# Second cross-attention with the logits computed once and turned probabilities, and the last batch's layer norm of the first cross-attention moved into the local attention's first steps

## The chip, the cores and the metric

The kernel runs on one core of a Trainium2 chip. The metric is the device time of one execution in microseconds (us). Engines: TensorE (PE, with its weight loads PEld), VectorE (DVE), ScalarE (ACT), GpSimd (POOL) and SyncE (SP), which starts the transfers. A difference under 0.5% (9.7 us) can't be told from no change here.

## What is computed

Four batches of 512 tokens of 128 numbers pass through four blocks; each block reads the layer norm of the stream and adds its result to the stream.

```python
x = x + cross_attention(layernorm(x), ctx)        # part a
x = x + six_local_attention_layers(layernorm(x))  # part b: windows of 32, 16 heads, each with a gated FFN
x = x + second_cross_attention(layernorm(x), ctx) # part c
x = x + mixture_of_8_experts(layernorm(x))        # part c
```

The second cross-attention, of which the change rewrites the softmax (77 context rows, 16 heads of 8 numbers):

```python
qp = q @ Wq.T
scores = qp @ kv.T ; idx = argmax(scores, -1)
mem = kv[idx] ; mk, mv = split(mem @ Wkv.T, 2)
logits = (qh @ mk.T) / sqrt(8)
attn = softmax(logits, -1)
out = (attn @ mv) @ Wc.T
```

Since every row of `mem` is one of the 77 context rows, the kernel counts how often each row is picked (a one-hot matrix, summed by PE) and works on 77 keys with their counts.

## The kernel before

The program has three parts, each a block in which the five engines run their own instruction lists in order and meet through semaphores; between the parts all engines meet. The residual stream lies in `residual` (X), the normalised stream in `stream` (XS), both 128 partitions wide with 16 tiles of 128 tokens. A tile is called u (0 to 15), a batch b has four.

Part a (`cross_attention`) ends, for every batch, with `residual(b)` on DVE (the sum, then the statistics), `second(b)` on POOL (variance plus epsilon, then the power -1/2) and `stream(b)` on DVE (subtract the mean, multiply). Batch 3 is last: nothing else is left when its chain runs.

Part b (`windowed_layers`) begins with small fills and tables. POOL waits for four transfers (`const_in`, two of them the query and key scales, two the layer norm's gain and bias) before it makes the rotary table of layer 0. PE's `enter(b)` transposes the normalised stream of batch b; `enter(3)` comes only in the third turn of four tiles. Each engine follows a written list (`PE_TURN`, `ACT_TURN`, `DVE_TURN`, `POOL_TURN`). Near its end part b also prepares batch 0 of the second cross-attention (the functions `first_...`): `first_queries` on ACT copies the queries from PSUM three times, whole and in two halves, `low` and `high`.

Part c (`gathered_mixture`) is a software pipeline over tiles. In iteration u, PE computes the logits of tile u+1 (L2449, four groups of four heads, 128 tokens by 308, one PSUM bank each), the probabilities of tile u, the attended values of tile u-1 (L2472, and `by_token` L2480, which turns them back to tokens) and the output of tile u-2. The softmax works so: DVE takes the maximum of each head over 77 keys (`highest`, L2094). PE turns these negative maxima (L2455), ACT copies them (L1935) into rows of `low` and `high`, which hold the queries of half of the heads each. PE then computes the logits a second time, turned (keys on the partitions) and with the maximum already subtracted, since the maxima stand among the rows of the product (`probs_t`, L2464, four groups). ACT takes the exponential as it reads them from PSUM (L1941) into `probs_t`. DVE's `shares` (L2100, L2105) divides by the sum.

Beside this every batch has pieces that share the bank of the fourth logits group (`bk_p`): `normed`, `queries`, `scores`, `counts` for the next batch, and `route`, `affine`, `rank` for tiles that are done. A piece in iteration u waits on PE until DVE has read the logits of tile u+1:

```python
def piece_bank(kind, b):
    wait(pe, piece_done, nth[kind, b] - 1)
    if (kind, b) in where:
        pe.wait_ge(lmax_done, 4 * min(where[kind, b] + 2, NT))
```

DVE's order in an iteration is: `highest(u+1)`, `residual(u-2)`, the statistics of finished tiles, `best` (the argmax and the one-hot, L2064), `keys`, `shares(u-1)`, and the rest. After `highest`, `best` and `shares` of one iteration PE still has `counts`, the last group of `probs_t` and `attended_tt` (L2485, which needs `shares(u-1)`) before the next logits.

## Time and profile before

| | |
|---|---|
| median of 3 runs | 1940.81 us (1939.25 to 1948.31) |
| profiled execution | 1946.22 us, its span 1944.0 us |
| part a, from the span's start to the meeting | 0 to 68.1 us |
| part b | 68.1 to 1715.1 us |
| part c, cross-attention iterations 0 to 15 | 1715.1 to about 1868 us |
| part c, the rest | to 1944.0 us |
| mean granted clock of PE | 0.973 |

The profile gives for every engine the time in which it worked; a share near 1 tells where work may bound a stretch, and the timeline and the waits tell what an idle engine waited for. "Granted clock" is the share of PE's 2.4 GHz that it was given: 1.00 or 0.50.

### The profile page before, as it was taken

To read this page: it belongs to the slowest core of one execution; us is meant where nothing else is said; L and a number is where in the kernel's file an instruction comes from. 1 tells how busy PE (TensorE), PEld (TensorE's weight loads), DVE (VectorE), ACT (ScalarE), POOL (GpSimd) and SP (SyncE) were. 2 spreads that over 40 slices of the span, in tenths; PEclk is the share of its full clock that TensorE was granted. 3 is DMA by queue.
4 is the path that set the end of the run, shared out by engine and by line. 5 is a ranking of instruction groups with operands and counts; after the bars stand their busy time and mean duration, and the time that the engine had idled before them with its cause. 6 is when DMAs were issued, how large, how long until landed. Compare 5 with 4: busy or idle time off the path is not lost. (4 is left out here: it accounts for less than half of the span.)

```text
span 1944.0 us, 78927 instructions
## 1 busy us (share of the span) xinstructions
PE 1819.9 (94%) x32815; PEld 1274.1 (66%) x32815; DVE 1433.7 (74%) x2623; ACT 1140.1 (59%) x2387; POOL 1438.3 (74%) x1838
## 2 busy tenths in 40 slices
PE   7689999999999999999999999999999999789878
PEld 6356667666666666666666766666666666566668
DVE  4587777877787778778777877888778878355556
ACT  2266566656666665666566666656666666334434
POOL 2588779878888888888788888888888879222334
PEclk9799999999999999999999999999999999889979
DMA  3111311111311113111122111121111101030012
GB/s 103 30 52 44 103 49 49 52 45 48 102 54 49 41 47 103 53 45 52 48 67 85 51 41 45 35 88 33 28 35 37 39 24 36 10 100 1 20 44 67
DMA packets 60837, 99.93 MB, mean 51 GB/s; under 512 B 15848, under 2 KB 35065, under 8 KB 58643
## 3 DMA queue, kind: packets, MB, share of 16 engines
q1 hardware_dynamic: 58978, 91.72, 16.3%
q8 instruction: 262, 4.29, 1.0%
q0 software_dynamic: 1504, 3.17, 0.5%
q14 instruction: 93, 0.75, 0.1%
HBM read 44.50 MB, written 21.45 MB: 34 GB/s over the span
## 5 line engine op out<-in xcount | busy, mean ns | idle before, releaser
L1332 PE MATMUL b_bank_proj<-layer_weights,b_stream_t 128*128 128x512 f32 x1152 | 593.7, 617 | 12.5 <-DVE b_plain_moved L1128 9.3
L1128 DVE TENSOR_TENSOR b_plain_moved<-b_bank_proj,b_rope 128x1024 f32<-128x1024 f32 x384 | 467.4, 1221 | 110.3 <-ACT b_squares L962 107.0
L871 POOL TENSOR_TENSOR b_rotated<-b_plain_moved 128x1024 f32<-128x1024 f32 x192 | 453.7, 2363 | 46.5 <-DVE b_plain_moved L1128 46.5
L886 POOL TENSOR_TENSOR b_rotated<-b_rotated,b_inv_norm 128x1024 f32<-128x1024 f32 x192 | 365.5, 1904 | 15.2 <-POOL b_inv_norm L882 0.2
L962 ACT ACTIVATE b_squares<-b_bank_proj 128x512 f32<-128x512 f32 x384 | 229.3, 597 | 248.3 <-PE b_bank_proj L1332 245.3
L1332 PEld LDWEIGHTS b_bank_proj<-layer_weights,b_stream_t 128*128 128x128 f32 x1152 | 188.7, 192 | 115.3 <-issue 53.2
L1134 DVE TENSOR_REDUCE b_norm<-b_squares 128x16 f32<-128x1024 f32 x192 | 232.2, 1209 | 42.7 <-ACT b_squares L962 42.5
L1340 PEld LDWEIGHTS b_bank_shared<-const_tables,b_rotated 128*128 128x128 f32 x1536 | 181.5, 143 | 72.9 <-issue 68.8
L1340 PE MATMUL b_bank_shared<-const_tables,b_rotated 128*128 128x128 f32 x1536 | 213.1, 277 | 3.4 <-POOL b_rotated L886 1.6
L891 POOL TENSOR_TENSOR b_probs<-b_probs,b_inv_sum 128x512 f32<-128x512 f32 x192 | 200.8, 1049 | 14.4 <-DVE b_inv_sum L1149 14.3
L1406 PEld LDWEIGHTS b_bank_shared<-b_attended_t,layer_weights 128*128 128x128 f32 x1536 | 184.2, 193 | 24.9 <-issue 23.2
L1406 PE MATMUL b_bank_shared<-b_attended_t,layer_weights 128*128 128x128 f32 x1536 | 188.5, 276 | 1.6 <-ACT b_attended_t L999 1.6
L1140 DVE TENSOR_REDUCE b_max<-b_bank_scores 128x8 f32<-128x512 f32 x192 | 130.0, 677 | 80.4 <-PE b_bank_scores L1365 80.2
L999 ACT ACTIVATE b_attended_t<-b_bank_shared 128x512 f32<-128x512 f32 x192 | 106.7, 595 | 98.9 <-PE b_bank_shared L1394 97.4
L969 ACT ACTIVATE b_v<-b_bank_proj 128x512 f32<-128x512 f32 x192 | 114.7, 597 | 83.3 <-PE b_bank_proj L1332 80.6
L1365 PE MATMUL b_bank_scores<-b_k_t,b_q_t 64*32 64x64 f32 x12288 | 146.6, 224 | 14.5 <-issue 11.8
L1365 PEld LDWEIGHTS b_bank_scores<-b_k_t,b_q_t 64*32 64x32 f32 x12288 | 140.4, 105 | 24.5 <-issue 16.1
L1394 PEld LDWEIGHTS b_bank_shared<-b_probs_t,b_v_shifted 64*64 64x64 f32 x6144 | 98.4, 134 | 71.9 <-issue 71.1
L1437 PE MATMUL b_bank_proj<-b_normed_t,layer_weights 128*128 128x512 f32 (+1 forms) x288 | 144.1, 616 | 1.1 <-issue 0.6
L1142 DVE TENSOR_TENSOR b_bank_scores<-b_bank_scores,b_max 128x512 f32<-128x512 f32 x192 | 134.3, 700 | 6.6
L1394 PE MATMUL b_bank_shared<-b_probs_t,b_v 64*64 64x32 f32 x6144 | 115.2, 221 | 25.5 <-issue 25.5
L1375 PEld LDWEIGHTS b_bank_shared<-const_tables,b_probs 128*128 128x128 f32 x768 | 94.4, 143 | 64.3 <-issue 58.5
(367 smaller groups left out, 2896.7 us busy)
## 6 DMA issues: line engine op xcount, KB each, us to landing
b_v_shifted<-b_v SPq DMA_DIRECT2D x192, 192.0 KB, 2.4
sorted_rows<-sorted_rows SPq DMA_DIRECT2D x66, 258.0 KB, 3.2
layer_weights<-L_ffn_Wqkv SPq DMA_DIRECT2D x6, 1536.0 KB
b_v_shifted<-b_v SPq DMA_DIRECT2D x72, 128.0 KB, 3.0
layer_weights<-L_ffn_Wo SPq DMA_DIRECT2D x6, 512.0 KB
c_sorted_in<-sorted_rows SPq DMA_DIRECT2D x23, 129.0 KB, 2.2
layer_weights<-L_ffn_w SPq DMA_DIRECT2D x8, 256.0 KB, 5.8
c_w<-L_ffn_w SPq DMA_DIRECT2D x8, 256.0 KB, 5.7
```

The lines of the kernel that those rows point to most:

```text
L871: nc.gpsimd.tensor_tensor(out=turned[:, k, :], in0=pm[:, k, 0, :], in1=pm[:, k, 1, :], op=ALU.add).then_inc(add_done, 1)
L886: nc.gpsimd.tensor_tensor(out=tk, in0=tk, in1=repeat_last(rn[:, k, :], DH), op=ALU.mult).then_inc(rope_done, 1)
L891: nc.gpsimd.tensor_tensor(out=p, in0=p, in1=repeat_last(share[:, b, :], LOOK), op=ALU.mult).then_inc(p_done, 1)
L962: nc.scalar.activation(squares[:, (c % 2) * 512:(c % 2) * 512 + 512], bk_proj[c % 2][:, :], ACT.Square).then_inc(sq_done, 1)
L1128: nc.vector.tensor_tensor(to, src.to_broadcast(shape), tab.to_broadcast(shape), ALU.mult).then_inc(mul_done, 1)
L1134: nc.vector.tensor_reduce(ss[:, k, :], squares[:, :].rearrange("p (a h c) -> p h a c", a=2, h=HEADS), AX.XY, ALU.add).then_inc(ss_done, 1)
L1332: nc.tensor.matmul(out, xs[:, b, t * P:(t + 1) * P], w, start=True, stop=True).then_inc(proj_full, 1)
L1340: last = nc.tensor.transpose(bank[:, n * P:(n + 1) * P], turned[:, g // 2, at:at + P], ident)
L1365: last = nc.tensor.matmul(bk_s[r][to, at:at + LOOK], qT[rows, u % 2, p, w, :], kT[rows, p, t * P + w * WIN:t * P + w * WIN + LOOK], start= ...
L1394: last = nc.tensor.matmul(banks[r][h * HALF:(h + 1) * HALF, p * HALF + w * WIN:p * HALF + (w + 1) * WIN], (V2, V)[w][rows, t, head * DH:(h ...
L1406: last = nc.tensor.matmul(bank[:, 0:P], weights(l, W_O + n * P, P), OT[:, u % 2, n, :], start=(n == 0), stop=(n == PAIRS - 1))
L1437: nc.tensor.matmul(bk_proj[c % 2][0:w, :], weights(l, W_UP + at, w), xnT[:, :], start=True, stop=True).then_inc(up_full, 1)
```

## The change

1. Last layer norm of part a. Statistics, power and normalisation of batch 3 leave part a. In part b DVE's first instructions are the statistics, POOL does the two small ones after its fills, and DVE normalises after its tables. `enter(3)` waits for it. POOL's wait before the rotary table is now for the two scale transfers alone.
2. Softmax of part c. `highest` on DVE now also subtracts the maximum from each group of logits (PSUM) and writes the differences to a new tile `raised` in SBUF. ACT takes the exponential there, in place. PE transposes the four groups (16 transposes a tile), and ACT copies them from PSUM to `probs_t`. The turned maxima, their copies, `low` and `high`, their fills and the half copies of the queries are gone. A piece's wait (`lmax_done`) now ends with the subtraction.

```diff
 def highest(u):                                   # DVE
-    wait(dve, max_full, u - 1)
+    wait(dve, pT_full, 4 * (u - 1))
     for n, g in enumerate((0, 2, 1, 3)):
         dve.wait_ge(lg_full, 4 * u + n + 1)
-        nc.vector.tensor_reduce(nm[:, u % 2, at:at + GROUP], split(bk_l[g][:, 0:GROUP * CTX], CTX), AX.X, ALU.max,
-                                negate=True).then_inc(lmax_done, 1)
+        group = split(bk_l[g][:, 0:GROUP * CTX], CTX)
+        largest = nm[:, u % 2, g * GROUP:(g + 1) * GROUP]
+        nc.vector.tensor_reduce(largest, group, AX.X, ALU.max, negate=True).then_inc(max_done, 1)
+        dve.wait_ge(max_done, 4 * u + n + 1)
+        nc.vector.tensor_tensor(split(raised[:, u % 2, g, :], CTX), group, repeat_last(largest, CTX),
+                                ALU.add).then_inc(lmax_done, 1)
-def highest(u):                                   # ACT
-    act.wait_ge(max_full, u + 1)
-    for a in range(2):
-        last = nc.scalar.activation(stack(a, b)[maxes[a], t * P:(t + 1) * P], bk_l[0][maxes[a], 384:384 + P], ACT.Copy)
-    last.then_inc(max_done, 1)
+def exponent(u):                                  # ACT, in its place
+    for n, g in enumerate((0, 2, 1, 3)):
+        act.wait_ge(lmax_done, 4 * u + n + 1)
+        nc.scalar.activation(raised[:, u % 2, g, :], raised[:, u % 2, g, :], ACT.Exp).then_inc(raised_done, 1)
 def probs_t(u, q):                                # ACT
-    nc.scalar.activation(pT[:, u % 2, q, :], bk_t[q % 2][0:CTX, :], ACT.Exp).then_inc(pT_done, 1)
+    nc.scalar.activation(pT[:, u % 2, (0, 2, 1, 3)[q], :], bk_t[q % 2][0:CTX, :], ACT.Copy).then_inc(pT_done, 1)
 def probs_t(u, q):                                # PE
-    if q == 0:
-        pe.wait_ge(max_done, u + 1)
+    g = (0, 2, 1, 3)[q]
+    pe.wait_ge(raised_done, 4 * u + q + 1)
     wait(pe, pT_done, 4 * u + q - 1)
     for n in range(GROUP):
-        last = nc.tensor.matmul(bk_t[q % 2][0:CTX, n * P:(n + 1) * P], kbd[:, b % 2, a, h, :],
-                                stack(a, b)[:, t * P:(t + 1) * P], start=True, stop=True)
+        last = nc.tensor.transpose(bk_t[q % 2][0:CTX, n * P:(n + 1) * P], raised[:, u % 2, g, n * CTX:(n + 1) * CTX], ident)
@@ first_queries, and queries(b) alike
-    nc.scalar.activation(front.queries, bank[:, :], ACT.Copy)
-    nc.scalar.activation(front.low[sides[0], :], bank[sides[0], :], ACT.Copy)
-    nc.scalar.activation(front.high[sides[1], :], bank[sides[1], :], ACT.Copy).then_inc(fq_done, 1)
+    nc.scalar.activation(front.queries, bank[:, :], ACT.Copy).then_inc(fq_done, 1)
```

On PE, in part c, iteration 3 before, with one piece (`normed`, L2386); `c_low_queries_max` and `layer_weights` are where the stacked queries lie:

```order
L2449 MATMUL c_bank_logits<-c_keys_by_head,c_queries_t 128x308 x4
L2464 MATMUL c_bank_turned<-layer_weights,c_keys_by_head 77x128 x4
L2489 MATMUL c_bank_out<-layer_weights,c_attended_tt 128x128
L2464 MATMUL c_bank_turned<-layer_weights,c_keys_by_head 77x128 x4
L2472 MATMUL c_bank_attended<-c_probs_t,layer_weights 32x512 x4
L2464 MATMUL c_bank_turned<-layer_weights,c_keys_by_head 77x128 x4
L2480 MATMUL c_bank_out<-const_tables,c_attended_t 128x128 x4
L2386 MATMUL c_bank_logits<-const_tables,c_normed 128x128 x4
L2455 MATMUL c_bank_logits<-const_tables,c_neg_max 128x128
L2464 MATMUL c_bank_turned<-layer_weights,c_keys_by_head 77x128 x4
L2485 MATMUL c_bank_out<-const_tables,c_attended 128x128
```

The same iteration on PE after the change:

```order
L2458 MATMUL c_bank_logits<-c_keys_by_head,c_queries_t 128x308 x4
L2467 MATMUL c_bank_turned<-const_tables,c_raised 77x128 x4
L2491 MATMUL c_bank_out<-layer_weights,c_attended_tt 128x128
L2467 MATMUL c_bank_turned<-const_tables,c_raised 77x128 x4
L2474 MATMUL c_bank_attended<-c_probs_t,layer_weights 32x512 x4
L2467 MATMUL c_bank_turned<-const_tables,c_raised 77x128 x4
L2482 MATMUL c_bank_out<-const_tables,c_attended_t 128x128 x4
L2396 MATMUL c_bank_logits<-const_tables,c_normed 128x128 x4
L2467 MATMUL c_bank_turned<-const_tables,c_raised 77x128 x4
L2487 MATMUL c_bank_out<-const_tables,c_attended 128x128
```

The turned products have become transposes of `raised`, and the turned maxima (L2455) are gone; nothing else moved.

On DVE, at the meeting of part a and part b, before (`residual(3)` first):

```order
L375 TENSOR_TENSOR residual<-a_bank_n,residual 128x512
L378 BN_STATS a_stats<-residual 128x6 x4
L382 BN_AGGR a_mean_var<-a_stats 128x2 x4
L389 TENSOR_SCALAR stream<-residual,a_mean_var,a_rstd 128x128 x4
L199 UNCONDITIONAL_BRANCH
L1100 UNCONDITIONAL_BRANCH
L1102 MEMSET b_max 128x16
L1103 MEMSET b_sum 128x16
L1104 MEMSET b_mask_rows 128x16
```

And after, to the first instructions of the local attention:

```order
L375 TENSOR_TENSOR residual<-a_bank_n,residual 128x512
L199 UNCONDITIONAL_BRANCH
L1105 UNCONDITIONAL_BRANCH
L1109 BN_STATS b_last_stats<-residual 128x6 x4
L1113 BN_AGGR b_last_mean_var<-b_last_stats 128x2 x4
L1115 MEMSET b_max 128x16
L1116 MEMSET b_sum 128x16
L1117 MEMSET b_mask_rows 128x16
L1121 CAST b_mask_rows<-const_tables 32x32 x2
L1123 CAST b_mask_bands<-const_tables 128x1024
L1127 CAST b_mask_bands<-const_tables 128x2x64
L1131 TENSOR_SCALAR stream<-residual,b_last_mean_var,b_last_rstd 128x128 x4
```

The statistics and the normalisation stand behind the branch into part b, ahead of and behind DVE's fills and tables.

On DVE, at the reductions of two tiles in part c, after the change (before, one row of four reductions stands in the place of the first eight):

```order
L2102 TENSOR_REDUCE c_neg_max<-c_bank_logits 128x4
L2104 TENSOR_TENSOR c_raised<-c_bank_logits,c_neg_max 128x308
L2102 TENSOR_REDUCE c_neg_max<-c_bank_logits 128x4
L2104 TENSOR_TENSOR c_raised<-c_bank_logits,c_neg_max 128x308
L2102 TENSOR_REDUCE c_neg_max<-c_bank_logits 128x4
L2104 TENSOR_TENSOR c_raised<-c_bank_logits,c_neg_max 128x308
L2102 TENSOR_REDUCE c_neg_max<-c_bank_logits 128x4
L2104 TENSOR_TENSOR c_raised<-c_bank_logits,c_neg_max 128x308
```

Each reduction is now followed by a subtraction that waits for it.

## Rows read from the trace of the kernel before

**Rows 1.** The page, part 1: busy time and share of the span.

```profile
PE 1819.9 (94%) x32815; PEld 1274.1 (66%) x32815; DVE 1433.7 (74%) x2623; ACT 1140.1 (59%) x2387; POOL 1438.3 (74%) x1838
```

**Rows 2.** The timeline of PE, iteration 3 of part c (start, us, line, operands, count).

```profile
1749.06 1.31 PE L2449 MATMUL c_bank_logits<-c_keys_by_head,c_queries_t 64*128 64x308 f32 x8
...
1752.42 1.07 PE L2472 MATMUL c_bank_attended<-c_probs_t,layer_weights 77*32 77x512 f32 x8
1753.42 1.10 PE L2464 MATMUL c_bank_turned<-layer_weights,c_keys_by_head 128*77 128x128 f32 x8
1754.35 0.60 PE L2480 MATMUL c_bank_out<-const_tables,c_attended_t 128*128 128x128 f32 x4
1754.79 0.60 PE L2386 MATMUL c_bank_logits<-const_tables,c_normed 128*128 128x128 f32 x4
...
1756.65 1.31 PE L2449 MATMUL c_bank_logits<-c_keys_by_head,c_queries_t 64*128 64x308 f32 x8 [0.17 <-ACT c_high_queries_max L1935]
```

**Rows 3.** Busy time of each engine over fourteen iterations of part c (columns as in the page).

```profile
1733.60:1858.50 124.90, 112.98 (x901) 85.05 (x901) 66.17 (x299) 60.69 (x134) 33.60 (x40) 1.00 0.03 10
```

**Rows 4.** DVE timeline in part b: a reduction, the subtraction that needs it, what follows.

```profile
905.47 0.69 DVE L1140 TENSOR_REDUCE b_max<-b_bank_scores 128x8 f32<-128x512 f32 x1 [0.73 <-PE b_bank_scores L1365]
906.20 0.70 DVE L1142 TENSOR_TENSOR b_bank_scores<-b_bank_scores,b_max 128x512 f32<-128x512 f32 x1
906.81 0.86 DVE L1164 BATCH_NORM_STATS2 b_stats<-b_normed 128x6 f32<-128x128 f32 x4
```

**Rows 5.** Groups on DVE in part c: one with the shape of the new subtraction.

```profile
L2064 DVE TENSOR_TENSOR c_onehot<-const_tables,c_pick_f 128x308 f32<-128x308 f32 x3 | 1.4, 479 | 0.1
```

**Rows 6.** Groups on ACT in part c: one with the shape of the new exponential.

```profile
L1905 ACT ACTIVATE c_scores<-c_bank_logits 128x308 f32<-128x308 f32 x3 | 1.3, 428 | 1.8 <-PE c_bank_logits L2398 1.8
```

**Rows 7.** Timeline, iteration 5 of part c: DVE's reductions and one-hot, then PE's logits, counts and next logits.

```profile
1766.99 1.63 DVE L2094 TENSOR_REDUCE c_neg_max<-c_bank_logits 128x4 f32<-128x308 f32 x4 [2.33 <-PE c_bank_logits L2449]
...
1772.06 0.48 DVE L2064 TENSOR_TENSOR c_onehot<-const_tables,c_pick_f 128x308 f32<-128x308 f32 x1
...
1766.10 1.31 PE L2449 MATMUL c_bank_logits<-c_keys_by_head,c_queries_t 64*128 64x308 f32 x8
...
1772.69 1.09 PE L2406 MATMUL c_bank_logits<-c_onehot,const_tables 128*128 128x77 f32 x8 [0.69 <-DVE c_onehot L2064]
...
1775.75 1.31 PE L2449 MATMUL c_bank_logits<-c_keys_by_head,c_queries_t 64*128 64x308 f32 x8
```

**Rows 8.** The longest waits of DVE in those fourteen iterations (us, times, longest).

```profile
DVE c_neg_max L2094 <- PE c_bank_logits L2449: 25.6, 10, 8.0
...
DVE c_rows L2166 <- ACT c_ranks L1929: 9.6, 2, 6.3
DVE c_normed L2046 <- POOL c_rstd L1795: 4.4, 2, 2.8
```

**Rows 9.** Short stretches around falls of the granted clock (PEclk, third column from the end).

```profile
56.00:58.00 2.00, 0.15 (x1) 0.00 (x0) 1.85 (x10) 0.60 (x1) 0.57 (x1) 1.00 0.00 0
58.00:60.00 2.00, 1.94 (x12) 1.97 (x13) 0.84 (x4) 0.00 (x0) 1.04 (x2) 0.69 0.04 8
...
1865.00:1868.00 3.00, 1.57 (x11) 0.54 (x12) 1.48 (x10) 1.26 (x3) 0.00 (x0) 0.97 0.00 0
```

**Rows 10.** PE at the lower clock, the transposes of the last tile.

```profile
1867.91 1.11 PE L2480 MATMUL c_bank_out<-const_tables,c_attended_t 128*128 128x128 f32 x4 [0.72 <-ACT c_attended_t L1946]
```

**Rows 11.** Timeline from the end of part a to the first local attention.

```profile
62.64 0.69 DVE L375 TENSOR_TENSOR residual<-a_bank_n,residual 128x512 f32<-128x512 f32 x1 [2.37 <-PE a_bank_n L494]
...
66.12 1.12 DVE L389 TENSOR_SCALAR stream<-residual,a_mean_var,a_rstd 128x128 f32<-128x128 f32 x4 [1.48 <-POOL a_rstd L241]
...
68.12 1.28 ACT L938 ACT_TABLE_LOAD   x1 [11.33 <-PEq L103]
...
76.25 2.34 DVE L1128 TENSOR_TENSOR b_plain_moved<-b_bank_proj,b_rope 128x1024 f32<-128x1024 f32 x2
```

**Rows 12.** Timeline near the end of part b: PE waits for ACT's queries.

```profile
1703.83 1.09 PE L1509 MATMUL b_bank_shared<-layer_weights 128*128 128x77 f32 x8 [0.82 <-ACT layer_weights L1054]
```

More of the change, by code:

```diff
@@ L247, in _ @@
                     bias(b)
-                for b in range(B):
+                for b in range(B - 1):
                     second(b)
@@ L375, in residual @@
                     nc.vector.tensor_tensor(xb, bk_n[b][:, :], xb, ALU.add).then_inc(x_done, 1)
+                    if b == B - 1:
+                        return
                     dve.wait_ge(x_done, b + 1)
@@ L728, in windowed_layers @@
         rstd = m.sb("rstd", [P, TILES])
+        last_st = m.sb("last_stats", [P, TILES, 6])
+        last_mv = m.sb("last_mean_var", [P, TILES, 2])
+        last_ve = m.sb("last_var_eps", [P, TILES])
+        last_rs = m.sb("last_rstd", [P, TILES])
         xn = m.sb("normed", [P, TILES, P])
@@ L757, in windowed_layers @@
         ident = const[:, C_IDENT:C_IDENT + P]
-        NC = 4
+        NC = 2
         NF = 7
@@ L847, in _ @@
                 pool.wait_ge(pool_set, NP)
-                pool.wait_ge(const_in, 16 * NC)
+                pool.wait_ge(last_stats, 1)
+                nc.gpsimd.tensor_scalar(last_ve[:, :], last_mv[:, :, 1], EPS, None, ALU.add).then_inc(last_ve_done, 1)
+                pool.wait_ge(last_ve_done, 1)
+                nc.gpsimd.tensor_tensor(out=last_rs[:, :], in0=last_ve[:, :], in1=mhalf[:, 0:TILES], op=ALU.pow).then_inc(last_rstd_done, 1)
+                pool.wait_ge(scale_in, 32)
                 def table(l):
@@ L908, in first_fill @@
                     nc.gpsimd.memset(front.v32, 0.0).then_inc(f_set, 1)
-                    nc.gpsimd.memset(front.low, 0.0).then_inc(f_set, 1)
-                    nc.gpsimd.memset(front.high, 0.0).then_inc(f_set, 1)
                 def first_rstd():
@@ L1101, in _ @@
             def _(dve):
+                before = (B - 1) * SEQ
+                for t in range(TILES):
+                    last = nc.vector.bn_stats(last_st[:, t, :], cols(X, before + t * P, P))
+                last.then_inc(last_st_done, 1)
+                dve.wait_ge(last_st_done, 1)
+                for t in range(TILES):
+                    last = nc.vector.bn_aggr(last_mv[:, t, :], last_st[:, t, :])
+                last.then_inc(last_stats, 1)
                 nc.vector.memset(top[:, :, :], 0.0).then_inc(b_set, 1)
@@ L1114, in _ @@
                 nc.vector.tensor_copy(bands16[:, 1, :, 0, 0, :], band.to_broadcast([P, 2, LOOK])).then_inc(band_set, 1)
+                dve.wait_ge(last_rstd_done, 1)
+                dve.wait_ge(last_stats, 1)
+                for t in range(TILES):
+                    last = nc.vector.tensor_scalar(cols(XS, before + t * P, P), cols(X, before + t * P, P), last_mv[:, t, 0:1],
+                                                   last_rs[:, t:t + 1], ALU.subtract, ALU.mult)
+                last.then_inc(last_done, 1)
                 def mul(u, c):
@@ L1310, in enter @@
                     take(bank, x0_done, b + 1)
+                    if b == B - 1:
+                        pe.wait_ge(last_done, 1)
                     for t in range(TILES):
@@ L1596, in gathered_mixture @@
         qpT = m.sb("queries_t", [P, B - 1, SEQ])
-        low = m.sb("low_queries_max", [P, B - 1, SEQ])
-        high = m.sb("high_queries_max", [P, B - 1, SEQ])
+        raised = m.sb("raised", [P, 2, GSIZE, GROUP * CTX])
         sc = m.sb("scores", [P, TILES * CTX])
@@ L1721, in queries_of @@
             return qpT[:, b - 1, :] if b else front.queries
-        def stack(a, b):
-            return (low, high)[a][:, b - 1, :] if b else (front.low, front.high)[a]
         first = [lot.start for lot in LOTS]
@@ L1851, in _ @@
                 by_head(0)
-                nc.gpsimd.memset(nm[:, :, :], 0.0).then_inc(nm_set, 1)
                 inverse(1)
-                nc.gpsimd.memset(low[:, :, :], 0.0).then_inc(low_set, 1)
-                nc.gpsimd.memset(high[:, :, :], 0.0).then_inc(low_set, 1)
                 nc.gpsimd.memset(cum[:, 0, :], 0.0).then_inc(cum_set, 1)
@@ L1896, in queries @@
                     act.wait_ge(piece_full, nth["queries", b])
-                    act.wait_ge(low_set, 2)
-                    nc.scalar.activation(queries_of(b), bk_p[:, :], ACT.Copy).then_inc(q_done, 1)
-                    nc.scalar.activation(stack(0, b)[sides[0], :], bk_p[sides[0], :], ACT.Copy)
-                    nc.scalar.activation(stack(1, b)[sides[1], :], bk_p[sides[1], :], ACT.Copy).then_inc(piece_done, 1)
+                    nc.scalar.activation(queries_of(b), bk_p[:, :], ACT.Copy).then_inc(piece_done, 1)
                 def scores(b):
@@ L2004, in _ @@
                     if u + 1 < NT:
-                        highest(u + 1)
+                        exponent(u + 1)
                     if u < NT:
@@ L2395, in scores @@
                     piece_bank("scores", b)
-                    pe.wait_ge(q_done, b)
+                    pe.wait_ge(piece_done, nth["queries", b])
                     for t in range(TILES):
@@ L2442, in logits @@
                         wait(pe, v_done, b)
-                    for g in (0, 2, 1, 3):
+                    for n, g in enumerate((0, 2, 1, 3)):
                         rows_ = sides[g // 2]
-                        if g == 0:
-                            wait(pe, max_done, u)
+                        wait(pe, lmax_done, 4 * (u - 1) + n + 1)
                         if g == 3:
```

41 lines of the change are left out of this document (14 added, 27 removed).

## The prediction

> **What bounds the kernel now.** I read the page first: PE works for 94% of the span, DVE for 74%, ACT for 59% [rows 1]. An average over three parts says little of a change to single steps, so I went on to PE's timeline of part c, where the softmax is. The reader should look at the start times there: each row of PE begins as the one before it stops issuing, from one logits row at 1749.06 to the next at 1756.65, 7.6 us, with one wait of 0.17 us [rows 2]. Over fourteen iterations PE is busy for 113.0 of 124.9 us at a granted clock of 1.00, DVE for 66.2, ACT for 60.7 [rows 3]. So PE sets the pace of this stretch. DVE's waits say the same from the other side: it waited 25.6 us there for PE's logits [rows 8]. At the end of part a the opposite holds: one chain DVE, POOL, DVE runs with all else idle, and part b starts behind it [rows 11].
>
> **The layer norm of batch 3.** The residual sum ends at 62.64 + 0.69 = 63.33, the last normalisation at 66.12 + 1.12 = 67.24, and part b begins 0.9 us later [rows 11]. With the chain moved, part b begins 0.9 us after 63.33: **-3.9 us**. The chain is not gone, it runs in part b beside other work. DVE's share of it (3.9 us less POOL's piece and the sum) is done well before its first product at 76.25, which is 8.1 us after the start of part b; before that DVE has only fills, tables and one reduction of squares [rows 11]. POOL's two small instructions stand before the rotary table. Even if the table came at its old time, that product would start no later. The table may come earlier by the shorter wait, but PE, ACT and the reduction of squares end at that same 76.25, so I take nothing for it. `enter(3)` is two turns later. If this cover failed (the table late), the loss would be what POOL is late, at most the 2.6 us between the sum's end and the start of the last normalisation (2.8 us).
>
> **The first queries.** PE waits 0.82 us for ACT's three copies before the scores of batch 0 [rows 12]. Two of them go: **-0.8 us**, if the rest of that chain shifts with it; between 0 and that.
>
> **PE in part c.** A turned group of eight instructions takes 1754.35 - 1753.42 = 0.93 us, four transposes take 1754.79 - 1754.35 = 0.44 us [rows 2]. Four groups a tile: 4 x (0.93 - 0.44) = 1.96 us less, and with the transpose of the maxima (a quarter of 0.44) 2.07 us. Over the fourteen iterations PE's work falls from 113.0 to 84 us.
>
> **DVE in part c.** No row shows a subtraction of 128x308 from PSUM with a broadcast second operand. The nearest two are the one-hot, the same shape from SBUF at 0.48 us [rows 5], and part b's subtraction of 128x512 in PSUM at 0.70 us [rows 4]. The bounds are 0.48 and 0.70; I take 0.48, since in part b the PSUM operand makes 0.70 out of 512 columns, 0.22 for 204 columns more. A reduction alone is then 0.69 - 0.22 = 0.47. The dependent subtraction starts 0.04 after its reduction ends (905.47 + 0.69 against 906.20), and an independent instruction overlaps the one before by 0.09 (906.20 + 0.70 against 906.81) [rows 4]. So a group takes 0.47 + 0.04 + 0.48 - 0.09 = 0.90 and a tile 3.6 us, where four reductions took 1.63 [rows 7]: **+2.0 us of DVE a tile**, +28 us in fourteen, 66 to 94 us.
>
> **ACT in part c.** Four exponentials of 128x308, each at 0.43 as the copy of that shape [rows 6], +1.7 us a tile; the four reads of the turned bank stay, as copies. 60.7 + 24 = 85 us less the copies of maxima and half queries: below the span. ACT is not the bound, but its exponentials of tile u+1 stand in its queue ahead of the last copy of tile u, and `counts` ahead of them.
>
> **What the stretch will take.** DVE becomes the longest. Two handovers lie open between PE and DVE in every iteration: from the logits' start to the first reduction, 1766.99 - 1766.10 = 0.89 us [rows 7], and from `shares` over the small transpose to the next logits, about 0.4 (estimate: one transpose's 0.27 to 0.3 latency and the semaphore). An iteration with little DVE work, like iteration 3, takes DVE 0.9 + 3.6 + 0.8 (residual and shares, estimate) + 0.4 = 5.7 us and PE 7.6 - 2.1 = 5.5: about 1.8 us gained. But most iterations carry extra DVE work ahead of `shares`. Iteration 5 is the example: the reductions end at 1768.62, the one-hot at 1772.54, PE's counts start 0.15 later and the next logits at 1775.75, 9.65 us after its own [rows 7]. After the change: 0.89 + 3.6 + 3.92 (unchanged, from the reductions to the one-hot) + 0.15 + 3.06 less 0.49 (the last turned group) and less 0.34 (maxima turned and copied) = 10.8. That is 1.1 us **longer**: PE's saving lies in DVE's shadow, DVE's addition lies on the path. A piece in the middle of PE's queue is also held until the subtraction is done, 2.0 us later than the reductions are now.
>
> The sum over fourteen iterations: DVE's work 94; open handovers 14 x 1.3 = 18, of which some 6 lie beside work that stands behind `shares`; DVE's waits for ACT's ranks and POOL's power, 9.6 + 4.4 = 14 now [rows 8], I take 12 (the first shrinks with PE's and ACT's queues, the second grows as DVE is later busy); waits behind `counts`, three times 2. 94 + 12 + 12 + 6 = 124 against 124.9 now: **-1**, uncertain by 5. Iteration 15, which has no logits and little DVE work, keeps PE's saving: **-2**. Iteration 0 has PE's second logits and the first piece behind DVE's longer pass: **+1**. Together with -3.9 and -0.8: -6.7 us.
>
> **The clock.** PE will be busy for 84 of 124, 68% instead of 90% [rows 3], and pause in one piece: in iteration 5 it is through with `by_token` some 5 us after its start and has nothing until 8.4. What pauses do is in the trace: with 0.15 us of work in 2 us the clock still stood at 1.00, and in the next 2 us it was 0.69, on its way to 0.50; after a stretch of 1.57 busy of 3 us it fell too [rows 9]. Four transposes at 1.2 GHz took 1.11 us where they take 0.60 at 2.4 [rows 10, 2]. On the path of an iteration like 5 the lower clock adds about 0.5 to the first logits, 1.7 to the counts and 0.5 to the last group: 2.7 us. I take four such iterations (three of the nine loaded ones have a pause over 3 us, and one more in the rest): **+11 us**. Behind this trace stands the Trainium skill, "TensorE: Matmul & The Clock Gate", section "HAM oscillation — how this bites in real kernels": waits between bursts of matmuls throttle PE again and again. By that rule alone every loaded iteration would fall, which is the second rival below.
>
> **Sum.** -6.7 + 11 = +4. The profiled execution took 1946.22 us, 5.4 above the median of the three runs; the difference is put on the median, 1940.8: **1945 us**, +0.2%.
>
> **Rivals.**
> - *The clock holds.* Today's pauses of PE in part c leave it at 1.00 throughout [rows 3]. Then -6.7: 1934 us. Against it: the pauses get longer. Chance 0.15, a third of it past 0.5%.
> - *DVE is not the bound.* If DVE's passes hide as they do now, PE's saving counts in full: 14 x 2.07 = 29 and -6.7 + 1 for the rest, and with some falls of the clock -20: 1921 us. For it speak 58 us of idle time on DVE [rows 3]; against it that iteration 5 has the one-hot before PE's counts already now, with PE waiting 0.69 us for it [rows 7]. Chance 0.12.
> - *PE stays at 1.2 GHz through the loaded iterations.* Nine of them at 2.7 us are 24 us: -6.7 + 24 = +17, 1958 us. It decides from about six slow iterations on (-6.7 + 16 = +10). For it: once fallen, PE after 1868 was busy for half of the time and stayed low [rows 10]; against it: an iteration is denser than that. Chance 0.28.
> - *My forecast*, DVE takes over the pace and some falls of the clock eat what parts a and b gain: 0.45.
>
> **Chances.** A measurement here tells 0.5% (9.7 us) from no change. Faster: 0.05 + 0.12 = 0.17. Within: 0.45 + 0.10 = 0.55. Slower: 0.28. The range reaches to the cases on both sides: from 1928 (between the first two rivals; with the subtraction at its cheap end) to 1960 (the third rival, or the subtraction at 0.70 us, which would add 14 x 4 x 0.22 = 12 us).
>
> **What would show it.** Part b starts near 64.2 us and its first product 8.1 us later (step 1). In part c PE's busy time over iterations 1 to 14 is near 84 us, DVE's near 94, a group's reduction and subtraction start 0.9 us apart; iteration 5 is longer than 9.65 us, iteration 3 shorter than 7; the wait "logits for DVE" shrinks and PE waits for `raised` or `shares`. The granted clock dips between 1735 and 1860. I am wrong if the fourteen iterations take under 115 us or over 140, if the clock shows no dip, or if part b's start brings back a wait for the table.

## The result, and the profile after

The changed kernel took 1953.91 us in the median of 8 runs (1948.16 to 1960.64), the kernel before 1942.25 us (8 runs). The ratio is 1.0065, with a 95% interval of 1.005 to 1.0081: 12.6 us slower, between 9.7 and 15.7. The stated range, 1928 to 1960 us, held it. The likeliest case, no change within 0.5%, just missed it: 12.6 us lies above the 9.7 us that count as no change, and that outcome had a chance of 0.28.

The profiled execution is the fastest of the eight, 1948.16 us with a span of 1946.4. Its page, part 1 [answers to rows 1]:

```profile
PE 1811.8 (93%) x32543; PEld 1254.6 (64%) x32543; DVE 1465.5 (75%) x2687; ACT 1147.5 (59%) x2411; POOL 1431.5 (74%) x1833
```

DVE has 32 us more, PE 8 us less, and no share has moved by over two points. What happened stands in the stretches. The first is the timeline after at the start of part b and at its end [rows 11, 12]:

```profile
63.54 0.69 DVE L375 TENSOR_TENSOR residual<-a_bank_n,residual 128x512 f32<-128x512 f32 x1 [2.32 <-PE a_bank_n L495]
65.15 0.87 DVE L1109 BATCH_NORM_STATS2 b_last_stats<-residual 128x6 f32<-128x128 f32 x4 [0.91 <-PEq L103]
...
67.98 1.12 DVE L1131 TENSOR_SCALAR stream<-residual,b_last_mean_var,b_last_rstd 128x128 f32<-128x128 f32 x4
...
73.23 2.35 DVE L1147 TENSOR_TENSOR b_plain_moved<-b_bank_proj,b_rope 128x1024 f32<-128x1024 f32 x2
...
1687.16 1.01 PE L1530 MATMUL b_bank_shared<-layer_weights 128*128 128x77 f32 x8
```

Part b starts 0.92 us after the sum's end (64.23), its first product 8.08 us later, and the scores of batch 0 no longer wait. From the sum's end to the first product it is 9.00 us, where it was 12.92 [rows 11]. The second stretch is part c, iterations 1 to 14, in the windows [rows 3]:

```profile
1717.32:1861.02 143.70, 110.56 (x664) 72.66 (x663) 94.44 (x355) 69.04 (x160) 33.71 (x40) 0.84 0.02 8
```

It takes 143.7 us where it took 124.9, DVE is busy for 94.4 and the granted clock is 0.84 in place of 1.00. The groups on DVE there, by line and form [rows 5, 7]:

```profile
L2104 DVE TENSOR_TENSOR c_raised<-c_bank_logits,c_neg_max 128x308 f32<-128x308 f32 x56 | 26.8, 478 | 1.9
L2102 DVE TENSOR_REDUCE c_neg_max<-c_bank_logits 128x4 f32<-128x308 f32 x56 | 26.3, 470 | 27.0 <-PE c_bank_logits L2458 26.9
L2136 DVE TENSOR_SCALAR stream<-residual,c_route_mean_var,c_route_rstd 128x128 f32<-128x128 f32 x12 | 5.7, 537 | 0.0
```

The subtraction takes 478 ns: the cheap end of its bounds was the right one. The longest waits of DVE and PE there [rows 8]:

```profile
DVE c_neg_max L2102 <- PE c_bank_logits L2458: 26.9, 10, 6.5
PE c_bank_out L2482 <- DVE residual L2120: 8.8, 7, 4.1
PE c_bank_logits L2427 <- DVE stream L2136: 8.0, 3, 3.5
...
PE c_bank_logits L2416 <- DVE c_onehot L2073: 7.7, 3, 2.9
DVE c_normed L2055 <- POOL c_rstd L1812: 6.0, 2, 3.2
DVE c_rows L2176 <- ACT c_ranks L1940: 5.7, 2, 4.3
```

PE now waits 24.5 us in three places for DVE. In the kernel before they were short:

```profile
PE c_bank_logits L2417 <- DVE stream L2126: 5.5, 3, 1.8
PE c_bank_logits L2406 <- DVE c_onehot L2064: 1.4, 2, 0.7
PE c_bank_out L2480 <- DVE residual L2110: 0.5, 1, 0.5
```

Two rows of PE's timeline after show the clock. Four groups of logits take 1.31 us at the full clock; here they do not:

```profile
1790.87 2.42 PE L2458 MATMUL c_bank_logits<-c_keys_by_head,c_queries_t 64*128 64x308 f32 x8
...
1834.06 1.31 PE L2458 MATMUL c_bank_logits<-c_keys_by_head,c_queries_t 64*128 64x308 f32 x8
```

Of the fourteen iterations 1 to 14, seven begin with logits of 2.1 to 2.4 us. That counts only where a fall reaches the start of an iteration. Read iteration by iteration, the granted clock is below 1.00 in thirteen of the fourteen; these are iterations 3 and 4:

```profile
1736.67:1745.46 8.79, 8.65 (x43) 5.29 (x43) 5.31 (x15) 2.79 (x5) 1.19 (x2) 0.65 0.00 0
1745.46:1753.58 8.12, 7.26 (x50) 4.64 (x50) 4.89 (x12) 5.36 (x14) 0.00 (x0) 1.00 0.01 2
```

One thing must be kept apart from the change. Part b's windows of the two profiles, before and after, from its start to the first logits of part c:

```profile
68.00:1718.11 1650.11, 1575.39 (x31096) 1076.45 (x31096) 1272.77 (x1932) 1022.40 (x2091) 1342.69 (x1719) 0.98 0.18 51
```

```profile
65.00:1701.36 1636.36, 1568.68 (x31096) 1071.51 (x31096) 1274.27 (x1945) 1020.63 (x2089) 1340.73 (x1719) 0.99 0.18 51
```

The same 31096 products took 13.75 us less. That is not the change's: from DVE's first product to the first logits it is 1641.9 and 1628.1 us here, and anything from 1631.4 to 1641.7 in the profiles of the experiments, with no order between kernels with and without the change. So the two profiled executions, 2 us apart, hide a part c that is 19 us longer (from its first logits to the end: 225.9 and 245.0 us). All comparisons below are of part c, or of ratios over many runs.

### The profile page after: what moved, and what is told of

It is laid out like the page before. It is cut to its first block and busy times, and to the rows that moved or that the text cites. A ratio compares the mean times of both kernels' runs of the same rounds, so it can differ in the third digit from the quotient of the medians.

```text
span 1946.4 us, 78523 instructions
## 1 busy us (share of the span) xinstructions
PE 1811.8 (93%) x32543; PEld 1254.6 (64%) x32543; DVE 1465.5 (75%) x2687; ACT 1147.5 (59%) x2411; POOL 1431.5 (74%) x1833
## 3 DMA queue, kind: packets, MB, share of 16 engines
q1 hardware_dynamic: 58978, 91.72, 16.1%
## 5 line engine op out<-in xcount | busy, mean ns | idle before, releaser
L1353 PEld LDWEIGHTS b_bank_proj<-layer_weights,b_stream_t 128*128 128x128 f32 x1152 | 187.8, 191 | 114.1 <-issue 53.6
L1386 PEld LDWEIGHTS b_bank_scores<-b_k_t,b_q_t 64*32 64x32 f32 x12288 | 140.4, 105 | 20.4 <-issue 11.5
L1161 DVE TENSOR_TENSOR b_bank_scores<-b_bank_scores,b_max 128x512 f32<-128x512 f32 x192 | 134.3, 699 | 6.6
L1415 PE MATMUL b_bank_shared<-b_probs_t,b_v 64*64 64x32 f32 x6144 | 114.1, 220 | 23.1 <-issue 23.0
```

The source lines that it names most:

```text
L1353: nc.tensor.matmul(out, xs[:, b, t * P:(t + 1) * P], w, start=True, stop=True).then_inc(proj_full, 1)
L1386: last = nc.tensor.matmul(bk_s[r][to, at:at + LOOK], qT[rows, u % 2, p, w, :], kT[rows, p, t * P + w * WIN:t * P + w * WIN + LOOK], start= ...
L1415: last = nc.tensor.matmul(banks[r][h * HALF:(h + 1) * HALF, p * HALF + w * WIN:p * HALF + (w + 1) * WIN], (V2, V)[w][rows, t, head * DH:(h ...
```

## The experiments

"The thirteen iterations" are those from the logits of tile 2 to the logits of tile 15 (iterations 1 to 13), which every kernel has. Columns: the median and, beside it, that of the kernel before from the same series (it moves by up to 3.5 us between series, so the ratio is what compares), the ratio over all runs, and from the profile the time of the thirteen iterations, DVE's busy time in them and the granted clock.

| kernel | median / before's, us | ratio (95% interval) | thirteen, us | DVE, us | clock |
|---|---|---|---|---|---|
| before | 1942.25 | 1 | 115.3 | 61.4 | 1.00 |
| after | 1953.91 / 1942.25 | 1.0065 (1.005 to 1.0081) | 134.3 | 87.9 | 0.83 |
| e1, norm only | 1938.68 / 1942.11 | 0.9981 (0.9963 to 0.9999) | 115.3 | 61.4 | 1.00 |
| e2, softmax only | 1963.03 / 1942.11 | 1.0115 (1.009 to 1.0139) | 133.9 | 87.9 | 0.83 |
| e3, filled too long | 1956.33 / 1942.11 | 1.007 (1.0046 to 1.0095) | 139.3 | 88.2 | 0.96 |
| e4, padded | 1950.41 / 1942.11 | 1.0055 (1.0036 to 1.0075) | 132.3 | 87.7 | 0.94 |
| e5, one maximum per group | 1934.67 / 1943.65 | 0.9967 (0.9948 to 0.9986) | 118.1 | 62.2 | 0.87 |
| e6, subtraction twice | 1991.60 / 1943.65 | 1.0258 (1.0232 to 1.0284) | 157.3 | 108.3 | 0.79 |
| e7, before with subtraction | 1966.36 / 1943.65 | 1.0123 (1.0099 to 1.0146) | 136.8 | 88.3 | 0.93 |
| e8, filled | 1949.34 / 1945.63 | 1.0005 (0.9982 to 1.0028) | 124.1 | 88.1 | 0.97 |
| e9, e5 in another order | 1939.19 / 1945.63 | 0.9963 (0.9946 to 0.9981) | 120.9 | 61.5 | 0.89 |
| e10, e9 filled | 1934.90 / 1945.63 | 0.9946 (0.9917 to 0.9974) | 115.0 | 60.9 | 0.96 |
| e11, residual between | 1958.53 / 1942.76 | 1.0084 (1.0055 to 1.0114) | 133.7 | 88.4 | 0.85 |
| e12, e10, later norm | 1924.15 / 1942.76 | 0.99 (0.9872 to 0.9929) | 110.8 | 61.0 | 0.97 |

**The two halves, e1 and e2.** e1 is the kernel before with the hunks of the layer norm, e2 with those of the softmax.

> The kernel before with only the layer norm of batch 3 moved. Both theories: part b starts 3.9 us earlier and the time falls by 3.9 us, to about 1938 (ratio 0.998). A rival for this part, that the rotary table or the first product waits again, gives part of it back: 1940 to 1942.

> The kernel before with only the softmax change. If the whole loss comes from part c (19 us more between the first logits and the end in the profile after), and 0.8 us is saved at the first queries: 1942 + 16 to 18 = 1958 to 1960 (ratio 1.008 to 1.009). If the change of the median has another source (the earlier start, or spread of part b), the time is under 1950.

e1 took 1938.68 us against 1942.11: 3.7 us less by the ratio (0.2 to 7.2), and its thirteen iterations are those of before to 0.1 us. e2 took 1963.03 us, 22 us more by the ratio (17 to 27), with the same thirteen iterations as the whole change. The loss is all the softmax's. It is 5 us above what I expected, at the edge of the interval.

**The clock, e3 and e8.** Transposes (e3: products) of the identity ahead of PE's waits, into a bank that ACT has just read, in fourteen places (e3, where the expectation says thirteen) and fifteen (e8):

```diff
+                def fill(kind, u):
+                    count = FILL.get((kind, u), 0)
+                    if count:
+                        read, bank = {"logits": (4 * u - 1, 0), "back": (4 * u + 3, 0)}.get(kind, (4 * u + 2, 1))
+                        pe.wait_ge(pT_done, read)
+                    for _ in range(count):
+                        nc.tensor.transpose(bk_t[bank][:, 0:P], ident, ident)
@@ ahead of by_token, and alike in three other places
+                    fill("by_token", u)
                     if 1 <= u <= NT:
                         by_token(u - 1)
```

> The kernel after with idle PE time filled: in thirteen of PE's long pauses of part c 6 to 28 small products on the identity stand ahead of the wait, into a bank that nobody reads; they leave the result as it is. Theory 1 (the fallen clock is most of the loss, DVE's addition the smaller part): the granted clock stays near 1.00 over the fourteen iterations, which take about 130 us in place of 144, and the time is 1940 to 1943. Theory 2 (DVE's longer chain alone costs the time, PE's slower clock lies in its shadow): the clock holds and the time stays at 1952 to 1955. If the fillers themselves come onto the path, some 3 us more in either case.

> The kernel after with PE's pauses filled once more, now with 4 to 26 transposes of the identity per place (0.11 us each at the full clock, some three quarters of the pause that the profile after shows there). In the first filled kernel each filler took twice as long and 22 of them outlasted a pause of 2.9 us, so the time it gave back was spent again. Theory 1 (the fallen clock is a good part of the loss): granted clock near 1.00, the fourteen iterations take 132 to 137 us in place of 144, the time is 1941 to 1947. Theory 2 (DVE's chain alone): the clock holds and the iterations still take 142 us or more, the time is 1951 or more.

The windows of e3, and of e8, over the thirteen iterations:

```profile
1723.32:1862.57 139.25, 129.21 (x992) 101.09 (x991) 88.20 (x332) 65.47 (x152) 32.28 (x38) 0.96 0.03 9
```

```profile
1729.27:1853.34 124.07, 106.26 (x787) 75.26 (x786) 88.14 (x332) 65.31 (x152) 32.28 (x38) 0.97 0.03 10
```

In e3 the clock held, but PE was busy for 129 us: the fillers outlasted the pauses, and the run says nothing on the clock's price. In e8 they fit. The clock rose from 0.83 to 0.97 and the iterations fell from 134.3 to 124.1 us, by 10.2. The ratio fell by 0.006, 12 us, to 1.0005, which is 1943 us: theory 1. The fillers leave the other engines' work as it is, so that time is the lost clock's. The other 8.8 us over the 115.3 of before remain with the clock nearly whole. The split is not sharp: two of e8's iterations still begin with slow logits (4 and 7), and a filler may hold PE up a little, so the clock's part is 10.2 us or somewhat more.

**PE's saving, e4 and e7.** e4 makes each group of transposes twice. e7 is the kernel before, its subtraction goes to a spare tile:

```diff
@@ e4, probs_t on PE
-                    for n in range(GROUP):
+                    for n in [*range(GROUP), *range(GROUP)]:
@@ e7, highest on DVE
-                                                negate=True).then_inc(lmax_done, 1)
+                                                negate=True).then_inc(each_max, 1)
+                        count = 4 * u + (0, 2, 1, 3).index(g) + 1
+                        dve.wait_ge(each_max, count)
+                        nc.vector.tensor_tensor(split(spare[:, count % 2, :], CTX), split(bk_l[g][:, 0:GROUP * CTX], CTX),
+                                                repeat_last(nm[:, u % 2, at:at + GROUP], CTX), ALU.add).then_inc(lmax_done, 1)
```

> The kernel after with each of the four groups of transposes made twice, so that PE's work of a tile is 1.76 us longer (4 x 0.44), about as long as before the change. If PE's saving lies in DVE's shadow, as I argued, and the longer work also keeps the clock up: between 1945 and 1956. If PE's length is on the path and its clock plays no part: 1954 + up to 25 = 1970 to 1979.

> The kernel before with DVE's subtraction added (into a spare tile that nobody reads) and the bank released behind it, but with PE's two computations of the logits, turned maxima and all else as they were: DVE's price without PE's saving and without PE's pauses. PE is busy for 113 us as before, so the clock should stay at 1.00. If PE's saving is worthless in the new kernel and the clock is what costs: +8 to +15, 1950 to 1957. If PE's saving did pay for most of DVE's addition: +20 to +28, 1962 to 1970.

e4 took 1950.41 us, as the first theory had it. It gives PE 13 x 1.76 = 23 us more to do and takes 2 us less than the kernel after: the padding costs no more than its clock (0.94) gives back. Beside e8 it is 8.2 us longer at nearly the same clock. So about a third of PE's saving counts, and the rest lies in DVE's shadow (PE would only have waited for DVE that much longer). e7 shows DVE's addition without any saving, 21.5 us over the thirteen iterations for 27 us of added work:

```profile
1737.79:1874.56 136.77, 115.53 (x840) 86.76 (x840) 88.27 (x332) 56.68 (x124) 32.36 (x38) 0.93 0.03 9
```

The time fits the second theory. PE's saving paid for up to 21.5 - 8.8 = 13 of it, about half of the 13 x 2.07 = 27, more than I argued; part of both differences may be the clock, which is 0.97 in e8. But the clock was to stay at 1.00 in e7, since PE has all of its old work, and it fell to 0.93. So DVE's longer pass makes PE pause enough for that by itself, and the smaller load of PE is not the only reason for the fall. What e7 has beyond e4 (4.5 us) may be the way of the turned maxima, which also went; no run has that alone.

**The dose, e6.** A second subtraction ahead of each:

```diff
+                        nc.vector.tensor_tensor(split(spare[:, u % 2, :], CTX), group, repeat_last(largest, CTX), ALU.add)
                         nc.vector.tensor_tensor(split(raised[:, u % 2, g, :], CTX), group, repeat_last(largest, CTX),
                                                 ALU.add).then_inc(lmax_done, 1)
```

> The kernel after with every subtraction made twice on DVE (the first into a spare tile, before the signal): 64 more of 0.40 to 0.48 us, 26 to 31 us more of DVE's work. If DVE's passes lie on the path in nearly every iteration: 1954 + 22 to 30 = 1976 to 1984. If only the loaded iterations depend on DVE: 1954 + 8 to 15.

20.4 us more of DVE's work made the thirteen iterations 23.0 us longer, at a clock of 0.79. Each microsecond added to `highest` is now paid about in full, the further loss of clock (from 0.83) included. By the ratio it is 37 us in all, 7 above what I expected at most. In the profile the rest of part c has 10.7 more, 3.1 in iteration 0 and 7.6 behind the logits of tile 15. That last stretch differs by up to 5 us between the other profiles (92.8 to 98.1 us), so not all of it need be the edit's.

**The new wait, e11.** `residual(u-2)` releases the bank of `by_token` and stood behind the longer `highest`:

```diff
                     for n, g in enumerate((0, 2, 1, 3)):
+                        if n == 2 and between is not None:
+                            residual(between)
```

> The kernel after with DVE's residual sum of tile u-2 between the second and the third group of the maxima and subtractions, in place of behind the fourth. The profile after has a wait that my prediction did not count: PE's by_token stands 8.8 us in seven waits for that sum, which releases its bank, where before it was 0.5 us once. Theory A (this wait is part of the loss): the seven waits shrink to 2 or 3 us in all, iterations 2, 7, 11, 12 and 14 get 0.5 to 1.8 us shorter each, part c as a whole 4 to 7 us, the time is 1947 to 1950. Theory B (in each of these iterations DVE's later products end the iteration anyway): the waits move to the one-hot, the stream or the shares, and the time stays at 1952 to 1955.

The longest waits of PE in e11's thirteen iterations:

```profile
PE c_bank_logits L2418 <- DVE c_onehot L2073: 8.3, 3, 3.4
PE c_bank_logits L2429 <- DVE stream L2138: 7.3, 2, 3.9
PE c_bank_out L2489 <- DVE c_attended L2117: 3.1, 4, 1.2
...
PE c_bank_out L2484 <- DVE residual L2122: 1.8, 2, 1.3
```

The wait I went after fell from 8.0 us to 1.8. The one-hot's grew from 7.7 to 8.3, the stream's from 6.3 to 7.3, and the iterations took 133.7 us. The whole took 1958.53 us, the ratio agreeing with the kernel after (1.0084 against 1.0065). Theory B: it was where PE spent the time, not what cost it.

**Without the subtraction, e5 and e9.** One shift may serve all four heads of a group, and ACT can apply it as a bias while it reads PSUM:

```diff
@@ highest on DVE
-                        largest = nm[:, u % 2, g * GROUP:(g + 1) * GROUP]
+                        largest = nm[:, u % 2, g:g + 1]
@@ exponent on ACT
-                        nc.scalar.activation(raised[:, u % 2, g, :], raised[:, u % 2, g, :], ACT.Exp).then_inc(raised_done, 1)
+                        nc.scalar.activation(raised[:, u % 2, g, :], bk_l[g][:, 0:GROUP * CTX], ACT.Exp,
+                                             bias=nm[:, u % 2, g:g + 1]).then_inc(raised_done, 1)
```

The banks are then released by ACT (`raised_done`), so the exponentials stand ahead of the pieces' copies in its list.

> The kernel after without the subtraction on DVE: DVE takes one maximum per token for each group of four heads (a reduction of the same 308 columns), and ACT takes the exponential straight from PSUM with that maximum as its bias, ahead of its other copies. The shares are the same in exact arithmetic, since one shift serves all keys of a head. DVE's work over the fourteen iterations falls from 94 back to about 67 us, PE's stays at some 85 at the full clock, ACT's at 70. If the subtraction is the cause of the loss, directly and through the pauses it makes on PE: 1942 - 3.9 - 0.8 - 14 x 1.3 = 1918 to 1925. If the turned round over SBUF itself (DVE, ACT, PE with two more handovers) is the cause, whoever subtracts: 1940 to 1950.

> The kernel with one maximum per group and the exponential on ACT straight from PSUM, with the four exponentials behind ACT's second copy of turned probabilities in place of around its first (from iteration 1 on). In the profile of the former version ACT's first copy waited behind an exponential for a late maximum (iteration 7) and PE waited 1.5 us for that copy. If these waits matter: 2 to 5 us less than the former version's 1934.7, about 1931. If the exponentials are then late for the pieces, which wait for the bank: no change or 2 us more.

DVE is back at 62 us, and the whole gains 19 us on the kernel after, 16.1 of them in the thirteen iterations. With a median of 1934.67 us it beats the kernel before by 6.4 us (0.3%), clear of its interval but under 0.5%. That lies between the two theories. The subtraction was most of the loss, but the iterations take 118.1 us, 3 more than before and not 13 x 1.3 less, at a clock of 0.87: the gain over before lies outside them. What is left is not only the clock. ACT, whose exponentials now stand ahead of its other copies, keeps PE waiting for the turned attended values. In these iterations of the kernels before and after PE never waited for them:

```profile
PE c_bank_out L2485 <- ACT c_attended_t L1961: 9.0, 11, 1.5
```

e9 (forecast about 1931 us, 1935 by the ratio) changed nothing that can be told apart.

**With the clock, e10 and e12.** e10 is e9 with fillers (4 to 15 transposes in eleven places). e12 also moves one instruction list:

```diff
                     if 2 <= u < NT + 2:
                         residual(u - 2)
+                    if t == 3 and b + 2 < B:
+                        normalise(b + 2)
...
-                    if t == 2 and b + 2 < B:
-                        normalise(b + 2)
```

> The kernel of the run ahead (one maximum per group, exponentials behind the second copy) with PE's pauses of its loaded iterations filled by 4 to 15 transposes of the identity each. If the clock's falls (10 + 7 + 4 short ones of 3 us at half clock in the former profile) are what keeps this version from its gain in part c: 5 to 8 us less, 1924 to 1928. If they lie in DVE's and ACT's shadow: as without fillers, 1931.

> The kernel with one maximum per group, exponentials behind the second copy and filled pauses, with one more move: DVE normalises the next batch one iteration later, behind the maxima and the residual sum of iterations 3 and 7, so that it no longer waits 2.8 us for POOL's power with the maxima queued behind it. If that wait sets iteration 7 (12.5 us in the profile of the version without the move): 3 to 4 us less there, in all 1928 to 1932 (ratio 0.993). If the normalised rows are then late for PE's transposes in the same iteration: no gain, 1935.

The windows of e10, then of e12, over the thirteen iterations:

```profile
1716.41:1831.38 114.97, 95.55 (x692) 66.33 (x692) 60.93 (x280) 66.26 (x148) 33.03 (x38) 0.96 0.06 19
```

```profile
1717.70:1828.54 110.84, 93.96 (x693) 65.07 (x692) 61.01 (x280) 66.16 (x148) 33.08 (x38) 0.97 0.06 20
```

The fillers give 6.0 us in the profile; by the ratios e9 and e10 overlap. The later normalisation gives 4.1 us more, 3.8 of them in iteration 7 (12.5 to 8.7 us): DVE's wait for POOL's power, 3.9 us in e10, is 0.2 in e12. By the ratios e10 and e12 just overlap. e12 took 1924.15 us, the best version here, 1.0% under the kernel before.

## Why the prediction was right, and where not

**Layer norm.** Right: 3.9 us forecast, 3.9 in the profile after from the sum's end to the first product, 3.7 in e1 (0.2 to 7.2), and the cover held. For its failure the prediction names 2.6 and 2.8 us for the same stretch; by rows 11 it is 2.8.

**First queries.** The wait of 0.82 us is gone. No run had this edit alone.

**DVE in part c.** 94 us forecast, 94.4 measured; 0.90 us from one reduction to the next, as forecast. The sum of its busy time is right partly by luck, since it holds 2.3 us that I did not count (below). ACT came to 69 us. PE's busy time was to be near 84 us and reads 110.6: work at the lower clock takes longer. e8, less its 182 fillers at 0.12 us each, has about 92 (estimate from its 114.1), so in busy time PE saved some 21 us, not 29.

**What the stretch will take: the step that failed.** I forecast 124 us for iterations 1 to 14 at the full clock, -1 to before. e8, with the clock nearly whole, takes 133.0, +8. The kernel after, clock and all, takes 143.7 us, over the 140 that the prediction gives as a sign of being wrong. My sum had 30 us in which DVE does nothing, of them 12 for the handovers to PE and back; the kernel after has 143.7 - 94.4 = 49 us, e8 133.0 - 94.7 = 38. In e8 the waits for ACT's ranks and POOL's power are 11.7 us, as I took them (12). The handovers are what I sized wrong. Over the same iterations of e8 DVE's waits for PE add up to 25.6 us, where I had 12, or 18 with the waits behind `counts`:

```profile
DVE c_neg_max L2102 <- PE c_bank_logits L2468: 20.4, 10, 6.5
DVE c_inv_sum L2110 <- PE c_bank_out L2492: 5.2, 5, 1.9
```

DVE's wait for the logits was to shrink. It does with the clock nearly whole, from 25.6 to these 20.4 us, but in the kernel after it is 26.9. And PE waits not for `raised`, and only 3.4 us for `shares`, but for the residual sum, the stream and the one-hot. The timeline after, PE and DVE at the end of iteration 5 [rows 7], shows what the 1.3 us an iteration left out (the logits row is slow here, which lengthens DVE's wait):

```profile
1762.05 1.09 PE L2416 MATMUL c_bank_logits<-c_onehot,const_tables 128*128 128x77 f32 x8 [2.92 <-DVE c_onehot L2073]
...
1765.31 2.43 PE L2458 MATMUL c_bank_logits<-c_keys_by_head,c_queries_t 64*128 64x308 f32 x8
...
1766.81 0.48 DVE L2102 TENSOR_REDUCE c_neg_max<-c_bank_logits 128x4 f32<-128x308 f32 x1 [3.23 <-PE c_bank_logits L2458]
```

PE waits 2.9 us for the one-hot, and then DVE waits 3.2 us for PE's counts, last group and logits. Neither engine is the longest; in the iterations with pieces the two take turns, and the subtraction is one more turn. For iteration 5 the prediction had worked this chain out: 10.8 us, and e8 has 10.82. The sum over fourteen iterations then dropped it and took DVE's work and 1.3 us each. Iteration by iteration e8 less before reads +0.8, +1.7, +0.6, -0.7, +1.2, +0.8, +2.4, +0.3, +1.2, +0.8, -0.8, +0.7 and 0.0 for 1 to 13, in all +8.8. Iteration 3 was to be under 7 us and took 8.8 (8.2 in e8); 3 and 7 begin with DVE's `normalise`, which waits for POOL's power with `highest` behind it (6.0 us in two waits). Iteration 0 cost 0.4 us, not 1. Iteration 15 and all behind it gained 0.1, not 2: PE waits for ACT's copies there.

**The clock: right in sum, by luck.** +11 us forecast, 10.2 measured by e8. But I had four slow iterations at 2.7 us each. Seven of the logits rows are slow in the kernel after and two in e8, which makes 1.5 to 2 us for each; iteration 5 itself went from 10.82 us in e8 to 11.73. Falls come oftener than I took them to and cost less, as I read it because part of PE's slow work lies beside DVE's. The third rival's count, nine, was nearer than mine; its price, the same 2.7 us each, was as far off. That rival, not the second, is the one that the prediction ties to the rule of the Trainium skill ("TensorE: Matmul & The Clock Gate", section "HAM oscillation — how this bites in real kernels"), by which waits between bursts of matmuls throttle PE again and again. The trace agrees: the granted clock is below 1.00 in thirteen of the fourteen iterations. The prediction also says that PE after 1868 was busy for half of the time at the lower clock; the trace before has it busy for 14.4 of the 22 us to 1890.

**The sum.** -3.9 - 0.8 + 8.8 + 10.2 + 0.4 - 0.1 = +14.6 us, against 12.6 by the ratio. The difference to my +4 is mostly the stretch (9.8 us), then iteration 15 (1.9), not the clock. So the range held for a reason that it wasn't drawn for: its upper end stood for a clock loss of 24 us or a dearer subtraction, and what came was less than half of that clock loss, and the dependency between PE and DVE.

**The rivals.** "The clock holds" fell with the granted clock of 0.84. "DVE is not the bound" fell with e6. "PE stays at 1.2 GHz through the loaded iterations" foresaw +17 us, 1958 us, and stands nearer to the measured 12.6 us, 1953.9, than my forecast of +4, 1945; but its 24 us for the clock were 10.2.

**Left open.** Why e2 lies 5 us above what I expected of it; why e6's rest of part c grew by 10.7 us; how much of e5's 3 us over before is the clock's and how much ACT's; and how the 8.8 us divide between the late `residual`, `best` and stream, which e11 shows can't be taken one at a time.

## What to carry to other kernels

Moving work from a full engine to a half idle one gains only in those iterations in which the second one has slack (here 4 and 11). Work out the chain of each kind of iteration, both handovers and all, and add up the chains, not an engine's busy time. Before unloading TensorE, or lengthening what it waits for, ask whether it will then pause often enough to lose its clock; here that cost as much as the dependency itself. A shift that softmax doesn't care about can be made coarser until an instruction that runs anyway applies it, which beat both other ways. The price is in the numbers' range: the exponentials of a head whose logits all lie far below its group's maximum can vanish, and no run here tried such inputs.

## What the runs showed of the hardware that I had not expected

**DVE's normalisation is slower beside POOL's work.** The timeline after, in iteration 10, POOL and DVE:

```profile
1821.47 2.40 POOL L1819 TENSOR_TENSOR c_keys_by_head<-layer_weights 128x616 f32<-128x616 f32 x2 [11.74 <-DVE layer_weights L2092]
...
1821.93 2.54 DVE L2136 TENSOR_SCALAR stream<-residual,c_route_mean_var,c_route_rstd 128x128 f32<-128x128 f32 x4
```

And the kernel before in iteration 6, where the same four instructions came 2.1 us behind the start of POOL's two:

```profile
1780.08 2.40 POOL L1802 TENSOR_TENSOR c_keys_by_head<-layer_weights 128x616 f32<-128x616 f32 x2 [8.33 <-DVE layer_weights L2083]
...
1782.18 1.15 DVE L2126 TENSOR_SCALAR stream<-residual,c_route_mean_var,c_route_rstd 128x128 f32<-128x128 f32 x4
```

In iteration 6 of the kernel after they took 2.09 us. One instruction takes 339 ns in the median of the kernel after, and up to 1255; in the kernel before the longest took 392. Over iterations 1 to 14 the group went from 3.4 to 5.7 us, just ahead of PE's wait for the stream. The longer `highest` had taken up most of DVE's pause between `keys` and `shares` (1.68 us in iteration 6 before, 0.49 after), and so put the normalisation beside POOL's work. The Trainium skill has the rule ("SBUF — State Buffer", section "Who interferes with whom"): a `tensor_scalar` can take the port pair that DVE shares with GpSimd, and then whoever issues second is blocked for the whole of the other's instruction. The trace agrees in that one instruction of four lasts about as long as one of POOL's (1.25 us against 1.20). No run here separated the two engines to prove it.

**The clock falls without a long wait.** In iteration 12 of the kernel after PE's two waits were 1.66 and 1.17 us, with 1.5 us of work between them; the logits at its start took 1.31 us, those behind it 2.43:

```profile
1840.02 0.63 PE L2482 MATMUL c_bank_out<-const_tables,c_attended_t 128*128 128x128 f32 x4 [1.66 <-DVE residual L2120]
...
1842.66 0.47 PE L2487 MATMUL c_bank_out<-const_tables,c_attended 128*128 128x128 f32 x1 [1.17 <-DVE c_attended L2115]
1843.07 2.43 PE L2458 MATMUL c_bank_logits<-c_keys_by_head,c_queries_t 64*128 64x308 f32 x8
```

So a single wait need not be long for it.
